# Product-key retrieval in one pass over the table: the marks of the chosen keys, summed as ranks in rows and then turned

## The chip, the cores and the metric

One NeuronCore of a Trainium2 chip runs the whole program. The time is the device time of one execution in microseconds (us); of several executions the median is given. In the profile PE is the matrix engine TensorE (PEld its weight loads), DVE is VectorE, ACT is ScalarE, POOL is GpSimd, SP is SyncE, which here only issues DMAs.

## What is computed

A small network of four layers over 4 sequences of 576 tokens, 64 features each. The change lies in the first layer's feed-forward part, a retrieval with product keys, followed by an attention over what was retrieved:

```python
q = (x @ Wq_pk).reshape(b, n, P, HEADS, DIM_KEY).transpose(2, 0, 1, 3, 4)   # P = 2 sides, 8 heads
sim = jnp.einsum('pbnhd,pkhd->pbnhk', q, pk_keys)                            # 64 keys a side
scores, idx = jax.lax.top_k(sim, PK_TOPK)                                    # 16 a side
index = (idx[0][..., :, None] + 64 * idx[1][..., None, :]).reshape(b, n, HEADS, 256)
score = (scores[0][..., :, None] + scores[1][..., None, :]).reshape(b, n, HEADS, 256)
final_scores, pk_idx = jax.lax.top_k(score, FINAL_TOPK)                      # 16 of the 256 pairs
final_scores = jax.nn.softmax(final_scores, axis=-1)
k = jnp.einsum('bnhk,bnhkd->bnhd', final_scores, keys_table[ind])
v = jnp.einsum('bnhk,bnhkd->bnhd', final_scores, values_table[ind])
```

## The kernel before, in words

The tables are not gathered. `dense_rows_stage` runs over all 64 x 64 pairs of keys of a head as 32 chunks of 128 pairs (`CHUNKS`), with the tokens as columns. The 2304 tokens are 18 tiles of 128, in five groups of 2, 4, 4, 4 and 4 tiles (`GROUP_TILES`); a job is one head of one group, 40 jobs, 1280 chunks. A chunk has 256 columns in group 0 and 512 in the others.

The main loop, per chunk n: `spread_chunk(n)` on TensorE, two bf16 matmuls (L1180, L1181) that spread a token's marks and its logits over the 128 pairs; ScalarE's exponential E (L1289); VectorE's W (L1422), which keeps E where the sum of the two marks is above 16.5; `weigh_chunk(n - 2)` on TensorE, an f32 matmul in two passes (L1191) that adds table rows times W into a PSUM bank. TensorE issues `spread_chunk(n)` only when W(n - 2) is made (`w_made`), and every engine takes its instructions in the order in which they are written. SyncE loads a head's table (2 MB) per job and stacks marks and logits with 32 DMAs per job (`pile`).

The marks say which pairs are chosen. For each token, head and side, a key among the 16 best has a rank; a pair counts when the ranks of its two keys satisfy a limit. VectorE computes them in the generator `choose(t)` for tile t: similarities' maxima, indices and replacements in two rounds (20 steps; L1326, L1331, L1336), the pairs' choice, then for each of 8 heads a comparison that makes a one-hot (key, rank) of both sides (L1376) and a multiplication of the first side (L1380); then the sums and the logits (L1387, L1391, L1393), and, for a group's last tile, the logits less the logarithm of the sums (L1400). `mark(t, h)` on TensorE (L1155) turns and sums: 16 matmuls for each head, one per rank r, with the head's one-hot (128 tokens x 128, every 16th element) as weights and `ranked[:, r, :]`, the identity times 16 - r, as moving operand of 128 columns; they add into a quarter of PSUM bank 6 or 7. ScalarE copies four heads' marks at a time to bf16 (`copy_marks`, L1250). One-hots have two buffers: VectorE starts head h when the marks of head h - 2 are made.

The choice for the next group's tiles runs inside the current group's loop: each tile has a slot of 56 chunks. Within a slot one step of `choose` follows each W from chunk `CHOOSE_AT` = 4 on, the first head's comparison comes at chunk 33 (`ONEHOTS_AT`), head h's at 33 + 2h, TensorE's marks of head h at chunk 36 + 2h (`MARK_AT`), the logarithm at chunk 51 (`LOG_AT`). `project` and `sims` (L1136, L1146) are at chunks 0 and 2; `turn` (L1166) transposes the next job's logits at chunk 4 of each job. So there are 4 slots in group 0's loop, with 256 columns, and 12 in those of groups 1 to 3, with 512. The two tiles of group 0 itself are done ahead of the loop, each with project, similarities, choice and marks one after the other, with nothing beside them.

Of the kernel before, what the change touches and what calls it, by code (L numbers as in the profile page):

```python
# [25 lines left out]
P = 128  # L26
# [974 lines left out]
def dense_rows_stage(nc, core, I, norm, kept):  # L1001
# [7 lines left out]
    with Stage(nc, "pk") as at:  # L1009
# [12 lines left out]
        rest = at.sb("rest", [P, 2 * HEADS, KEYS])  # L1022
        vals = at.sb("vals", [P, 2 * HEADS, TOP])
        ids = at.sb("ids", [P, 2 * HEADS, TOP], U32)
# [11 lines left out]
        onehot = at.sb("onehot", [P, 2, 2, KEYS, TOP], BF16)  # L1036
# [6 lines left out]
        made = at.sb("made", [P, 2, BANK])  # L1043
        (consts, spread_made, xc_made, pk_made, pk_copied, sims_made, sims_copied, shifted, exped, summed, logged,
         onehots, marks_made, marks_copied, split, normal, turned, hi_made, left_made, mid_made, lo_made, x_made, e_made,
         w_made, acc_done, acc_copied, vec) = (at.sem(n) for n in (
            "consts", "spread_made", "xc_made", "pk_made", "pk_copied", "sims_made", "sims_copied", "shifted", "exped",
            "summed", "logged", "onehots_made", "marks_made", "marks_copied", "logits_made", "logits_normal", "logits_turned", "hi_made",
# [26 lines left out]
        with nc.Block() as block:  # L1075
# [53 lines left out]
            def _(pe):  # L1129
# [65 lines left out]
                for t in range(GROUP_TILES[0]):  # L1195
                    project(t)
                    sims(t)
                    for h in range(HEADS):
                        mark(t, h)
                turn(0)  # L1200
                total = len(jobs) * CHUNKS
                for n in range(total):
# [4 lines left out]
                    if t is not None:  # L1207
# [4 lines left out]
                        for h in range(HEADS):  # L1212
                            if i == MARK_AT[h]:
                                mark(t, h)
# [7 lines left out]
            def _(act):  # L1222
# [23 lines left out]
                def copy_marks(t, side):  # L1246
                    g = max(i for i in range(GROUPS_OF) if first_tile[i] <= t)
                    i = t - first_tile[g]
                    act.wait_ge(marks_made, HEADS * t + 4 * side + 4)
                    nc.scalar.activation(marks[:, g % 2, 4 * side:4 * side + 4, i * P:(i + 1) * P],  # L1250
                                         ps[:, 6 + side, :].rearrange("p (h n) -> p h n", n=P), ACT.Copy
                                         ).then_inc(marks_copied, 1)

# [21 lines left out]
                for t in range(GROUP_TILES[0]):  # L1275
# [3 lines left out]
                    copy_marks(t, 0)  # L1279
                    copy_marks(t, 1)  # L1280
# [3 lines left out]
                for n in range(len(jobs) * CHUNKS):  # L1284
# [8 lines left out]
                    if t is not None:  # L1293
# [19 lines left out]
            def _(dve):  # L1313
                steps = Steps(dve, vec)

                def choose(t):
# [7 lines left out]
                    for lo, of in ((0, X), (8, rest)):  # L1324
# [4 lines left out]
                        steps.settle()  # L1329
                        for q in range(2 * HEADS):  # L1330
# [42 lines left out]
                    for h in range(HEADS):  # L1373
                        if HEADS * t + h >= 2:
# [1801 lines left out]
```

## Time and profile before

| what | us |
|---|---|
| median of 3 runs | 4419.82 |
| lowest and highest | 4418.15 and 4446.55 |
| the profiled execution | 4430.5 |
| its span, first to last instruction | 4428.8 |
| PE, DVE, ACT busy in the span | 3578.2, 2649.8, 1444.5 |
| the retrieval's stage in the span (about) | 206 to 2139 |

The rows that follow the change come from that one profiled execution. Times are from the start of its span. A timeline row gives the start, the time that it covers, the engine, the line of the kernel, what is written from what, and how often the same stands in a row; in brackets the idle time ahead of it and what ended it. A matmul's row runs from its start to its modelled end; matmuls overlap, so the time that PE needs for one is read from the distance of starts.

### The profile page before, as it was taken

The page shows a single profiled execution, that of the slowest core. Times are in us where ns is not written, and L with a number is a line of the kernel's source. Part 1 is how long each engine was busy: PE and PEld are TensorE (multiplying, and loading weights), DVE is VectorE, ACT ScalarE, POOL GpSimd, SP SyncE. Part 2 cuts the span into 40 slices and gives each one's busy share as a digit, 9 for nine tenths or more (in the row PEclk, how much of TensorE's full clock was granted, in tenths as well). Part 3 has the DMA queues.
Part 4 walks back from the last instruction along what each step waited for, and adds up shares of the span by engine and source line. Part 5 has one row for each costly group of instructions (what it writes and reads, how often), then busy time and mean ns, then how long its engine had stood idle before and what let it go on. Part 6 is the DMA issues. An engine that isn't in the chain of part 4 may idle for free. (4 is left out here: it accounts for less than half of the span.)

```text
span 4428.8 us, 55552 instructions
## 1 busy us (share of the span) xinstructions
PE 3578.2 (81%) x16818; PEld 2073.3 (47%) x16818; DVE 2649.8 (60%) x7617; ACT 1444.5 (33%) x2746; POOL 351.8 (8%) x354
## 2 busy tenths in 40 slices
PE   5528889999999999999898978866769361899877
PEld 4325554544444454444466645543447241344354
DVE  3368878877887887555334331135455456999812
ACT  2203444444444444444334331013232134100023
POOL 1000000000000000000000001202000000345500
PEclk8569999999999999999879887977779675999968
DMA  0102343444344434444000020000000003100000
GB/s 7 53 10 70 100 99 84 101 89 93 86 100 93 87 82 102 100 111 94 19 20 22 20 85 0 1 4 1 13 19 0 2 0 74 24 0 0 0 7 6
DMA packets 140954, 207.89 MB, mean 47 GB/s; under 512 B 35104, under 2 KB 119657, under 8 KB 135469
## 3 DMA queue, kind: packets, MB, share of 16 engines
q1 hardware_dynamic: 140717, 205.03, 19.4%
q8 instruction: 111, 1.82, 0.2%
q14 instruction: 126, 1.03, 0.1%
HBM read 115.66 MB, written 10.03 MB: 28 GB/s over the span
## 5 line engine op out<-in xcount | busy, mean ns | idle before, releaser
L1191 PE MATMUL psum<-pk_W,pk_kv 128*128 128x512 f32 (+1 forms) x2560 | 1203.9, 552 | 10.0 <-issue 9.8
L1422 DVE SCALAR_TENSOR_TENSOR pk_W<-psum,pk_E 128x512 f32<-128x512 f32 (+1 forms) x1280 | 810.7, 633 | 440.3 <-ACT pk_E L1289 407.3
L1289 ACT ACTIVATE pk_E<-psum 128x512 f32<-128x512 f32 (+1 forms) x1280 | 709.1, 555 | 1004.7 <-PE psum L1181 1002.8
L1191 PEld LDWEIGHTS psum<-pk_W,pk_kv 128*128 128x128 f32 x2560 | 465.4, 191 | 173.7 <-issue 27.0
L1180 PE MATMUL psum<-pk_stack,pk_spread 128*128 128x512 bf16 (+1 forms) x1280 | 462.0, 361 | 90.3 <-DVE pk_W L1422 54.2
L2706 PE MATMUL psum<-tree_w,tree_x 128*128 128x512 bf16 x1728 | 383.4, 380 | 110.9 <-PEq L120 90.5
L1181 PE MATMUL psum<-pk_stack,pk_spread 128*128 128x512 bf16 (+1 forms) x1280 | 459.3, 359 | 0.0
L1180 PEld LDWEIGHTS psum<-pk_stack,pk_spread 128*128 128x128 bf16 x1280 | 125.1, 98 | 445.0 <-DVE pk_W L1422 349.5
L2706 PEld LDWEIGHTS psum<-tree_w,tree_x 128*128 (+1 forms) x1728 | 168.2, 99 | 312.5 <-issue 121.8
L2777 DVE COPY_PREDICATED leaf_acc<-leaf_path,psum 128x512 f32<-128x512 uint32 x468 | 310.2, 728 | 5.3 <-PE psum L2706 2.7
L1181 PEld LDWEIGHTS psum<-pk_stack,pk_spread 128*128 128x128 bf16 x1280 | 125.7, 98 | 241.9 <-issue 232.1
L1155 PEld LDWEIGHTS psum<-pk_ranked,pk_onehot 128*128 128x128 bf16 x2304 | 168.2, 149 | 115.4 <-issue 102.7
L1155 PE MATMUL psum<-pk_ranked,pk_onehot 128*128 128x128 bf16 x2304 | 172.0, 229 | 56.9 <-DVE pk_onehot L1380 56.9
L1125 POOL TENSOR_TENSOR pk_parts<-pk_left,pk_parts 128x512 bf16<-128x512 f32 (+1 forms) x40 | 44.0, 1099 | 1814.9 <-ACT pk_parts L1260 1814.9
L1376 DVE TENSOR_TENSOR pk_onehot<-pk_idf,pk_count 128x2048 bf16<-128x2048 bf16 x144 | 175.4, 1218 | 1.2 <-PE psum L1155 0.6
L295 PE MATMUL psum<-ident,xn 128*64 128x128 f32 x160 | 32.9, 396 | 171.6 <-DVEq L269 157.4
L881 ACT ACTIVATE peer_probs<-peer_probs,peer_stat 128x128 f32<-128x128 f32 (+4 forms) x160 | 96.3, 602 | 219.8 <-DVE peer_stat L916 219.4
L811 PE MATMUL psum<-peer_kv,peer_qT_padded 128*128 128x128 f32 (+4 forms) x320 | 160.4, 594 | 5.9 <-DVE peer_v L986 3.4
L913 DVE CUSTOM_DVE_ANT_0 peer_probs<-psum,peer_mask 128x128 f32<-128x128 f32 (+4 forms) x160 | 85.8, 536 | 113.3 <-PE psum L811 104.2
L1892 PE MATMUL psum<-moe_x,moe_w 128*85 x480 | 112.4, 385 | 43.6 <-PEq L120 42.2
L996 PE MATMUL psum<-peer_v,peer_pT 128*128 128x64 f32 (+2 forms) x960 | 138.5, 287 | 0.0
L2749 POOL TENSOR_TENSOR leaf_acc<-leaf_acc,leaf_of_level 128x512 f32<-128x512 f32 x90 | 90.5, 1039 | 536.6 <-DVE leaf_acc L2777 536.6
(534 smaller groups left out, 4770.2 us busy)
## 6 DMA issues: line engine op xcount, KB each, us to landing
pk_kv<-in_kv SPq DMA_DIRECT2D x40, 2048.0 KB, 8.1
pk_stack<-pk_parts SPq DMA_DIRECT2D x768, 64.0 KB, 2.5
pk_stack<-pk_marks SPq DMA_DIRECT2D x256, 64.0 KB, 2.6
peer_kv<-peer_kept SPq DMA_DIRECT2D x32, 288.0 KB, 2.8
peer_kept<-pk_made SPq DMA_DIRECT2D x32, 256.0 KB, 2.1
tree_weights_x<-in_tree_w SPq DMA_DIRECT2D x32, 256.0 KB, 4.5
pk_stack<-pk_parts SPq DMA_DIRECT2D x192, 32.0 KB, 2.0
dft_cos<-in_cos SPq DMA_DIRECT2D x1, 2596.5 KB
```

The lines of the kernel that those rows point to most:

```text
L811: last = nc.tensor.matmul(ps[0:r, bank, 0:min(w, BANK)], q, self.kT[:, u, 0:min(w, BANK)], start=True, stop=True)
L996: last = nc.tensor.matmul(ps[0:r, 1, c * d:(c + 1) * d], self.pT[0:k, self.pT_at[c] + m * r:self.pT_at[c] + (m + 1) * r], self.v1[0:k, u, ...
L1155: last = nc.tensor.matmul(ps[:, 6 + h // 4, h % 4 * P:(h % 4 + 1) * P], onehot[:, h % 2, :, :, r], ranked[:, r, :], start=(r == 0), stop=( ...
L1180: nc.tensor.matmul(ps[:, n % 2, 0:N], spread[:, 1, c % 2, :], of, start=True, stop=True)
L1181: nc.tensor.matmul(ps[:, 2 + n % 2, 0:N], spread[:, 0, c % 2, :], of, start=True, stop=True).then_inc(x_made, 1)
L1191: nc.tensor.matmul(ps[:, 4, 0:N], kv[:, k % 2, c, :], W[:, n % 3, 0:N], start=(c == 0), stop=(c == CHUNKS - 1)).then_inc(acc_done, 1)
L1289: nc.scalar.activation(E[:, n % 2, 0:width(k)], ps[:, 2 + n % 2, 0:width(k)], ACT.Exp).then_inc(e_made, 1)
L1376: steps.do(nc.vector.tensor_tensor(onehot[:, h % 2, :, :, :], idf[:, :, h, :].unsqueeze(2).to_broadcast([P, 2, KEYS, TOP]), count64[:, :, ...
L1422: nc.vector.scalar_tensor_tensor(W[:, n % 3, 0:width(k)], ps[:, n % 2, 0:width(k)], TOP + 0.5, E[:, n % 2, 0:width(k)], ALU.is_gt, ALU.mul ...
L1892: last = nc.tensor.matmul(ps[0:HALF, 3 * which + u % 3, :], w[:, lo:lo + HALF], x[:, bass.ds(g * BANK, BANK)], start=(k == 0), stop=(k == 2))
L2706: last = nc.tensor.matmul(ps[:, n % BANKS, :], x[:, bass.ds(t * P, P)], w[:, c * BANK:(c + 1) * BANK], start=(k == 0), stop=(k == len(prod ...
L2777: ins = nc.vector.copy_predicated(acc[:, u, level + 1, :, :], over(mask.bitcast(U32), D), bank)
```

## The change

A one-hot is now the moving operand. For each side (half of the heads, `side` 0 or 1) `rank(t, side)` runs 16 matmuls of 512 columns: the weights are `ranked[:, r, :]`, and the moving operand is every 16th element of four heads' one-hots. Their sum is a tile's ranks with the tokens as rows, in bank 6 or 7. ScalarE copies it as bf16 (`copy_ranks`), then `mark(t, side)` transposes the four heads' 128 x 128 blocks, and `copy_marks` copies them as before, from a bf16 PSUM bank. The one-hots have four buffers instead of two, and VectorE waits for the rank step of the half before when it starts a half. The sums and the logits stand between heads 3 and 4 instead of behind head 7. The first rank step stands at chunk 42 of a slot, its transposes at 44; the second at 52 and 54. To make room, `made` and the new `ranks` lie in the memory of `core.xn`, which is free in this stage, `rest` and `ids` in the first two one-hot buffers; before the second tile's and later tiles' indices VectorE waits for the last rank step of the tile before.

```diff
-        onehot = at.sb("onehot", [P, 2, 2, KEYS, TOP], BF16)
+        onehot = at.sb("onehot", [P, 4, 2, KEYS, TOP], BF16)
+        free = core.xn[:, :, :].rearrange("p t d -> p (t d)")
+        made = free[:, 0:2 * BANK].rearrange("p (k n) -> p k n", k=2)
+        ranks = free[:, 2 * BANK:2 * BANK + BANK // 2].bitcast(BF16)
+        rest = onehot[:, 0, :, :, :].rearrange("p s n r -> p (s n r)").bitcast(F32).rearrange("p (q n) -> p q n", n=KEYS)
+        ids = onehot[:, 1, 0, :, :].rearrange("p n r -> p (n r)").bitcast(U32)[:, 0:2 * HEADS * TOP].rearrange("p (q n) -> p q n", n=TOP)
...
-                def mark(t, h):
-                    if h == 0:
+                def rank(t, side):
+                    if side == 0:
                         pe.wait_ge(sims_copied, t + 1)
-                    pe.wait_ge(onehots, HEADS * t + h + 1)
+                    pe.wait_ge(onehots, HEADS * t + 4 * side + 4)
                     for r in range(TOP):
-                        last = nc.tensor.matmul(ps[:, 6 + h // 4, h % 4 * P:(h % 4 + 1) * P], onehot[:, h % 2, :, :, r],
-                                                ranked[:, r, :], start=(r == 0), stop=(r == TOP - 1))
+                        last = nc.tensor.matmul(ps[:, 6 + side, :], ranked[:, r, :],
+                                                onehot[:, :, :, :, r].rearrange("p h s n -> p (h s n)"),
+                                                start=(r == 0), stop=(r == TOP - 1))
+                    last.then_inc(ranks_made, 1)
+
+                def mark(t, side):
+                    pe.wait_ge(ranks_copied, 2 * t + side + 1)
+                    for h in range(4):
+                        last = nc.tensor.transpose(ps[:, 6 + side, :].bitcast(BF16)[:, h * P:(h + 1) * P],
+                                                   ranks[:, h * P:(h + 1) * P], ranked[:, TOP - 1, :])
                     last.then_inc(marks_made, 1)
...
-                        for h in range(HEADS):
-                            if i == MARK_AT[h]:
-                                mark(t, h)
+                        for side in range(2):
+                            if i == RANK_AT[side]:
+                                rank(t, side)
+                            if i == RANK_AT[side] + 2:
+                                mark(t, side)
...
+                def copy_ranks(t, side):
+                    act.wait_ge(ranks_made, 2 * t + side + 1)
+                    if t:
+                        act.wait_ge(marks_made, 2 * t + side - 1)
+                    nc.scalar.activation(ranks[:, :], ps[:, 6 + side, :], ACT.Copy).then_inc(ranks_copied, 1)
...
                     copy_sims(t)
                     exp_top(t)
-                    copy_marks(t, 0)
-                    copy_marks(t, 1)
+                    for side in range(2):
+                        copy_ranks(t, side)
+                        copy_marks(t, side)
...
-                            if i == MARK_AT[4 * side + 3] + 1:
+                            if i == RANK_AT[side] + 1:
+                                copy_ranks(t, side)
+                            if i == RANK_AT[side] + 3:
                                 copy_marks(t, side)
...
+                        if lo == 0 and t:
+                            dve.wait_ge(ranks_made, 2 * t)
                         for q in range(2 * HEADS):
                             steps.add(nc.vector.max_index(ids[:, q, lo:lo + 8], vals[:, q, lo:lo + 8], of[:, q, :]))
...
-                    for h in range(HEADS):
-                        if HEADS * t + h >= 2:
-                            dve.wait_ge(marks_made, HEADS * t + h - 1)
-                        steps.do(nc.vector.tensor_tensor(onehot[:, h % 2, :, :, :],
+                    def mark_head(h):
+                        if h % 4 == 0 and 2 * t + h // 4:
+                            dve.wait_ge(ranks_made, 2 * t + h // 4)
+                        steps.do(nc.vector.tensor_tensor(onehot[:, h % 4, :, :, :],
...
+
+                    for h in range(4):
+                        yield from mark_head(h)
                     dve.wait_ge(exped, t + 1)
...
                     yield
+                    for h in range(4, HEADS):
+                        yield from mark_head(h)
                     if t + 1 in first_tile:
...
-MARK_AT = [ONEHOTS_AT + 2 * h + 3 for h in range(HEADS)]
+RANK_AT = (ONEHOTS_AT + 9, ONEHOTS_AT + 19)
 EXP_AT = ONEHOTS_AT - 1
-LOG_AT = ONEHOTS_AT + 2 * HEADS + 2
+LOG_AT = ONEHOTS_AT + 11
```

## Rows read from the trace of the kernel before

**Rows 1.** The page, busy us of each engine (share of the span) xinstructions
```profile
PE 3578.2 (81%) x16818; PEld 2073.3 (47%) x16818; DVE 2649.8 (60%) x7617; ACT 1444.5 (33%) x2746; POOL 351.8 (8%) x354
```

**Rows 2.** Windows, 512-column loop: us, busy PE, PEld, DVE, ACT, POOL, PEclk, DMA, GB/s
```profile
1500.00:1600.00 100.00, 98.19 (x419) 49.14 (x418) 83.99 (x321) 45.09 (x77) 2.32 (x2) 1.00 0.40 90
```

**Rows 3.** Timeline inside a 512-column slot: start us, us, engine, line, operation, [idle before]
```profile
1640.98 0.38 PE L1180 MATMUL psum<-pk_stack,pk_spread 128*128 128x512 bf16 x1
...
1641.56 1.22 DVE L1376 TENSOR_TENSOR pk_onehot<-pk_idf,pk_count 128x2048 bf16<-128x2048 bf16 x1
...
1642.27 1.17 PE L1155 MATMUL psum<-pk_ranked,pk_onehot 128*128 128x128 bf16 x16
...
1642.81 0.69 DVE L1422 SCALAR_TENSOR_TENSOR pk_W<-psum,pk_E 128x512 f32<-128x512 f32 x1
...
1643.28 0.38 PE L1180 MATMUL psum<-pk_stack,pk_spread 128*128 128x512 bf16 x1
...
1643.42 0.68 DVE L1380 TENSOR_TENSOR pk_onehot<-pk_onehot,pk_depth 128x1024 bf16<-128x1024 bf16 x1
1643.49 0.38 PE L1181 MATMUL psum<-pk_stack,pk_spread 128*128 128x512 bf16 x1
...
1644.54 0.69 DVE L1422 SCALAR_TENSOR_TENSOR pk_W<-psum,pk_E 128x512 f32<-128x512 f32 x1 [0.44 <-ACT pk_E L1289]
1644.57 0.38 PE L1180 MATMUL psum<-pk_stack,pk_spread 128*128 128x512 bf16 x1
```

**Rows 4.** Timeline in the index lookups of the same slot, PE, ScalarE and VectorE
```profile
1605.33 0.60 ACT L1289 ACTIVATE pk_E<-psum 128x512 f32<-128x512 f32 x1 [0.71 <-PE psum L1181]
...
1605.98 0.39 PE L1180 MATMUL psum<-pk_stack,pk_spread 128*128 128x512 bf16 x1
...
1606.62 0.68 DVE L1422 SCALAR_TENSOR_TENSOR pk_W<-psum,pk_E 128x512 f32<-128x512 f32 x1
...
1607.36 0.39 PE L1180 MATMUL psum<-pk_stack,pk_spread 128*128 128x512 bf16 x1
```

**Rows 5.** Timeline inside a 256-column slot of group 0, VectorE and PE
```profile
385.98 1.22 DVE L1376 TENSOR_TENSOR pk_onehot<-pk_idf,pk_count 128x2048 bf16<-128x2048 bf16 x1
...
388.50 1.22 DVE L1376 TENSOR_TENSOR pk_onehot<-pk_idf,pk_count 128x2048 bf16<-128x2048 bf16 x1
...
393.97 0.28 PE L1180 MATMUL psum<-pk_stack,pk_spread 128*128 128x256 bf16 x1
...
394.63 0.27 PE L1180 MATMUL psum<-pk_stack,pk_spread 128*128 128x256 bf16 x1
```

**Rows 6.** Timeline of the first tile, ahead of the main loop
```profile
243.20 3.70 PE L1155 MATMUL psum<-pk_ranked,pk_onehot 128*128 128x128 bf16 x32 [25.39 <-DVE pk_onehot L1380]
...
250.28 0.60 ACT L1250 ACTIVATE pk_marks<-psum 128x512 bf16<-128x512 f32 x1 [10.01 <-PE psum L1155]
...
254.46 1.22 DVE L1376 TENSOR_TENSOR pk_onehot<-pk_idf,pk_count 128x2048 bf16<-128x2048 bf16 x1
...
256.32 0.28 DVE L1387 TENSOR_REDUCE pk_sums<-pk_fvals 128x8 f32<-128x128 f32 x1
...
256.52 0.68 DVE L1391 TENSOR_TENSOR pk_logits<-pk_sim,pk_vals 128x512 f32<-128x512 f32 x1
...
261.49 1.02 ACT L1234 ACTIVATE pk_sim<-psum 128x1024 f32<-128x1024 f32 x1 [2.08 <-PE psum L1146]
```

**Rows 7.** Windows view, 2 us of the first tile, columns as in rows 2
```profile
247.00:249.00 2.00, 1.57 (x16) 1.44 (x16) 1.97 (x4) 0.00 (x0) 0.00 (x0) 0.72 0.00 0
```

**Rows 8.** Source view, loads of the one-hots and of the spread matrix: ns min/median/max
```profile
L1155 PEld LDWEIGHTS psum<-pk_ranked,pk_onehot x2304: 140/148/171, 243.2 to 1748.0; 128*128 128x128 bf16 x192
...
L1180 PEld LDWEIGHTS psum<-pk_stack,pk_spread x1280: 95/98/152, 329.9 to 2134.8; 128*128 128x128 bf16 x183
```

**Rows 9.** Timeline of a later stage, PE, contiguous 128-column bf16 transposes
```profile
3084.94 0.22 PE L2066 MATMUL psum<-rot_soft_ident,rot_attn_q_parts 128*128 128x128 bf16 x1
...
3085.33 0.22 PE L2066 MATMUL psum<-rot_soft_ident,rot_attn_k_parts 128*128 128x128 bf16 x1
```

More of the change, by code:

```diff
@@ L1021, in dense_rows_stage @@
         sim = at.sb("sim", [P, 2, 2 * HEADS, KEYS])
-        rest = at.sb("rest", [P, 2 * HEADS, KEYS])
         vals = at.sb("vals", [P, 2 * HEADS, TOP])
-        ids = at.sb("ids", [P, 2 * HEADS, TOP], U32)
         idf = at.sb("idf", [P, 2, HEADS, TOP], BF16)
@@ L1042, in dense_rows_stage @@
         W = at.sb("W", [P, 3, BANK])
-        made = at.sb("made", [P, 2, BANK])
         (consts, spread_made, xc_made, pk_made, pk_copied, sims_made, sims_copied, shifted, exped, summed, logged,
-         onehots, marks_made, marks_copied, split, normal, turned, hi_made, left_made, mid_made, lo_made, x_made, e_made,
+         onehots, ranks_made, ranks_copied, marks_made, marks_copied, split, normal, turned, hi_made, left_made, mid_made, lo_made, x_made, e_made,
          w_made, acc_done, acc_copied, vec) = (at.sem(n) for n in (
             "consts", "spread_made", "xc_made", "pk_made", "pk_copied", "sims_made", "sims_copied", "shifted", "exped",
-            "summed", "logged", "onehots_made", "marks_made", "marks_copied", "logits_made", "logits_normal", "logits_turned", "hi_made",
+            "summed", "logged", "onehots_made", "ranks_made", "ranks_copied", "marks_made", "marks_copied", "logits_made", "logits_normal", "logits_turned", "hi_made",
             "left_made", "mid_made", "lo_made", "x_made", "e_made", "w_made", "acc_done", "acc_copied", "vector_steps"))
@@ L1211, in _ @@
                             sims(t)
-                        for h in range(HEADS):
-                            if i == MARK_AT[h]:
-                                mark(t, h)
+                        for side in range(2):
+                            if i == RANK_AT[side]:
+                                rank(t, side)
+                            if i == RANK_AT[side] + 2:
+                                mark(t, side)
                     k, c = n // CHUNKS, n % CHUNKS
@@ L1248, in copy_marks @@
                     i = t - first_tile[g]
-                    act.wait_ge(marks_made, HEADS * t + 4 * side + 4)
+                    act.wait_ge(marks_made, 2 * t + side + 1)
                     nc.scalar.activation(marks[:, g % 2, 4 * side:4 * side + 4, i * P:(i + 1) * P],
-                                         ps[:, 6 + side, :].rearrange("p (h n) -> p h n", n=P), ACT.Copy
+                                         ps[:, 6 + side, :].bitcast(BF16)[:, 0:BANK].rearrange("p (h n) -> p h n", n=P), ACT.Copy
                                          ).then_inc(marks_copied, 1)
+                def copy_ranks(t, side):
[3 more added lines that the diff above has]
+                    nc.scalar.activation(ranks[:, :], ps[:, 6 + side, :], ACT.Copy).then_inc(ranks_copied, 1)
                 def split_hi(k):
@@ L1278, in _ @@
                     exp_top(t)
-                    copy_marks(t, 0)
-                    copy_marks(t, 1)
+                    for side in range(2):
+                        copy_ranks(t, side)
+                        copy_marks(t, side)
                 log_sums(0)
@@ L1379, in choose @@
                         yield
-                        nc.vector.tensor_tensor(onehot[:, h % 2, 0, :, :], onehot[:, h % 2, 0, :, :],
+                        nc.vector.tensor_tensor(onehot[:, h % 4, 0, :, :], onehot[:, h % 4, 0, :, :],
                                                 rows_of(depth16[:, h, :], KEYS), ALU.mult).then_inc(onehots, 1)
                         yield
+                    for h in range(4):
+                        yield from mark_head(h)
                     dve.wait_ge(exped, t + 1)
```

1 line of the change is left out of this document (removed).

## The prediction, made before the changed kernel ran

> **What bounds the kernel now.** I read the page's busy times first, then the stretches, then the order of time inside one slot. PE is the busiest engine over the whole program, 81% [rows 1], but that is a mean over many stages. In the retrieval's main loop it is the bound almost alone: 98.19 of 100 us, at the full clock of 2.4 GHz [rows 2]. So in that loop an instruction taken from PE is worth its time, if nothing else comes up behind it.
>
> What stands behind it is seen in the order of time [rows 3]. Two chunks and one head's marks take 3.59 us of PE (1640.98 to 1644.57). A bare chunk takes 1.29 us (1643.28 to 1644.57), so the 16 matmuls of a head's marks take 3.59 - 2 x 1.29 = 1.01 us, 63 ns each. In the same 3.59 us VectorE makes one head's one-hots (1.25 us until the next instruction, then 0.60) and two W's (0.61 each), about 3.1 us, and only then waits 0.44 us. Without the mark between them two chunks are 2.58 us of PE against 3.1 us of VectorE: the marks of before stood exactly where VectorE needed the time. How far VectorE may be late is seen in the index lookups [rows 4]. There it takes 1.37 us a chunk; the W at 1606.62 is 0.69 us behind the end of its E (1605.93), and the spread that waits for it comes 1.38 us after the one before, 0.09 late. So about 0.6 us of lateness is free and the rest is PE's.
>
> In group 0 (256 columns) a chunk without other work is 0.66 us of PE (393.97 to 394.63), but two chunks with a head's one-hots take 2.52 us from one comparison to the next [rows 5], more than 2 x 0.66 + 1.01 = 2.33: VectorE is the bound there and the marks cost nothing.
>
> In the two tiles ahead of the loop everything is one chain. PE starts the marks cold: 32 matmuls in 3.70 us [rows 6], 107 ns each, at half clock, 1.2 GHz; the granted clock of the 2 us from 247 is 0.72 [rows 7], so the full level came at about 248.1, 4.9 us after the start.
>
> **The change part by part.** A tile's 128 matmuls of 128 columns become 32 of 512 columns (16 per rank step, two rank steps) and 8 transposes in bf16; ScalarE copies twice as often. The transposes are of the kind that runs every 56 ns (3084.94 to 3085.33, seven intervals) [rows 9]: 0.25 us a side with its start. ScalarE's extra 2 x 0.6 us [rows 6] lie in chunks where it works 0.6 of 1.29 us, and after the spread that follows the rank step PE has two weighs and a spread to do before it turns, 2.15 us, and ScalarE an exponential and the copy, 0.2 + 0.6 + 0.6 = 1.4: no wait in the loop.
>
> The unknown is the new matmul. A contiguous 512-column one takes 0.21 us of PE (the two spreads of a chunk start at 1643.28 and 1643.49 [rows 3]); that is the low end. But its moving operand is the one-hot at a step of 16 elements, 32 bytes, and no row has such a moving operand. The nearest is the same one-hot as weights [rows 8]: a load takes 148 ns against 98 for contiguous ones, and the pace is 63 ns per 128 columns against 56 [rows 3, 9]. Scaled by columns the pace gives 4 x 63 = 0.25 us, the whole duration of the load 4 x 148 = 0.59 us, the high end; between them lie the two f32 passes of the weigh, half of the chunk's other 0.86 us each, 0.43. I take 0.25, since a pace is what 16 in a row pay: 4.0 us per rank step.
>
> The Trainium skill speaks against the change here: "SBUF — State Buffer" (Door 1) says that reads at full bandwidth need at least two hits in each 16-byte line, so a bf16 step beyond 8 elements pays. The one-hot's slower loads agree in direction; no row shows the rate for a moving operand. It is the second case below.
>
> *Slots of 512 columns* (three groups of four tiles, 12 slots). Off PE: 8 x 1.01 = 8.1 us. Onto PE: 2 x (4.0 + 0.25) = 8.5. And four heads' one-hots now pass with no mark between: VectorE needs 4 x 3.1 = 12.4 us, PE 8 x 1.29 = 10.3; less the free 0.6 that is 1.5 us of PE waiting, twice a slot (the rank step lets VectorE catch up once, after each four), 3.0 us. Net 8.5 + 3.0 - 8.1 = +3.4, times 12 = +41 us.
>
> *Slots of 256 columns* (4). The first rank step starts about 0.9 us after W(40), when head 3 is ready; 4.0 us, then a spread, its semaphore and the E put W(43) 5.7 us after W(40). VectorE has 2.7 us of work for that time (a multiplication at 0.60, two W's at (2.52 - 1.25 - 0.60) / 2 = 0.33, the sums at 0.2, both logits at 0.6), so 3.0 us are new. The second rank step stands in light chunks, where VectorE has about 0.3 us left to do: 4.25 us less that and less the 0.6 that the last mark cost there, +3.4. Together +6.4, times 4 = +26 us.
>
> *The two tiles ahead of the loop.* VectorE reaches head 4 and waits for the first rank step, which can start only after head 3 (before, head 4 asked for head 2's marks); all of the tile's other work on VectorE is queued behind that wait, and the second rank step, the copies and the next tile's similarities wait for it. The step starts cold: 4.9 us at 0.43 us a matmul are 11, the other five at 0.25, 6.0 us in all; the sums and logits brought forward hide 1.4 us of it (0.2 + 0.6 + 0.6, as they are spaced from 256.32 on [rows 6]), 4.8 with the semaphore remain. After head 7 the next tile's similarities (261.49) waited for one mark of 1.2 us; now for a rank step, again cold after the 7.4 us of four heads (4 x 1.86, 254.46 to 256.32), a copy of 0.8 with its release and four slow transposes: 6.0 + 0.8 + 0.5 - 1.2 = +6.1. The second tile pays the same before the logarithm, which ScalarE issues behind its copies. 2 x (4.8 + 6.1) = +22 us.
>
> Other edits: `made`, `ranks`, `rest` and `ids` in borrowed memory change no shape. The wait in front of the second lookup's indices is long met in the loop, and ahead of it covered by the wait for the similarities. With `LOG_AT` earlier, VectorE's wait of about 1 us for the logarithm, once a group, goes; PE did not wait for it, so 0 (at most -4 us).
>
> **Sum.** +41 + 26 + 22 = +89 us. The profiled execution took 4430.5 us, span 4428.8; it would become 4519. The median of the runs is 4419.8, 10.7 lower, so I forecast 4509. With 0.21 us a matmul the three parts are 26 + 21 + 21 = +68 us, 4488.
>
> **The rivals.** About 1%, 44 us, is what a measurement here can tell from no change.
>
> 1. The strided stream runs at half rate, 0.43 us a matmul. For it: the one-hot's loads take half as long again as contiguous ones [rows 8]. Against it: their pace is only an eighth slower. A rank step is 6.9 us: 12 x (2 x 7.15 + 3.0 - 8.1) = 110, the narrow slots 4 x 12.1 = 48, the start 2 x (5.7 + 7.0) = 25. +183, 4603. At 0.59 us, the high end, it would be +279, 4699.
>
> 2. Not slower: VectorE's excess disappears. The place is the eight chunks before each rank step, the price 3.0 us a slot. It needs VectorE to have enough lateness free, 2.1 us instead of 0.6, from where PE's wait is 0, the matmul at 0.21, and the clock up during the first rank steps (3.4 us each). Then 12 x (7.3 - 8.1) = -9, narrow slots 4 x 3 = 12, start 2 x (2.2 + 3.5) = 11: +14, 4434, within 1%. Against it: 0.69 us of lateness already showed [rows 4]. For it: the count of PE's matmul time does go down.
>
> A page's figure would help this rival: the Trainium skill, "TensorE: Matmul & The Clock Gate" (Back-to-back issue gap), gives about 131 ns per sustained 512-column matmul, 2.1 us a rank step, by which rival 2 would come to about 4400. The trace disagrees: contiguous 512-column spreads come 0.21 us apart.
>
> 3. The waits bite in the loop (PE waiting for the copied ranks, VectorE for the rank step at head 4). By the order of issue both are met before they are asked; if the first cost 0.5 us a side, it would be 16 us more on the forecast, 4525, inside its range.
>
> **How the numbers follow.** Forecast with rival 3, 4470 to 4540: 0.50. Half rate or worse: 0.27. Rival 2: 0.15. A gain of over 1% needs -44 us, and the marks are about 8.1 x 12 = 97 us of the bound, so ranks almost free: 0.08. Slower by over 1% takes the first two, less a little: 0.75; within 1% 0.17; faster 0.08. The range holds rival 2's upper part and half rate: 4440 to 4620.
>
> **What would show it.** The new matmuls in the wide slots 0.25 us apart (0.21 or 0.43 decide between the cases). PE waiting for W in the eight chunks before each rank step, with chunks in pairs of 3.1 us; no such wait if rival 2 is right. A VectorE wait for the rank step of about 4 us in each of the first two tiles, and the second tile's similarities about 11 us later than 261.49. A wide slot with its 56 chunks 3.4 us longer than before. The forecast is wrong if wide slots come out shorter, or if PE's wait for W in the loop doesn't grow.

## The result, and the profile after

The changed kernel took 4939.31 us (median of 4 runs, 4937.59 to 4941.75), the one before 4425.59 in runs beside it: a ratio of 1.1161, interval 1.114 to 1.1182. It is some 510 us slower, where +89 was forecast, and it lies far above the range. The profiled execution took 4937.59 us with a span of 4935.7; the mean granted clock fell from 0.881 to 0.840.

The page's busy line, which answers to [rows 1]:

```profile
PE 4034.3 (82%) x15234; PEld 2011.3 (41%) x15234; DVE 2644.3 (54%) x7617; ACT 1463.0 (30%) x2782; POOL 356.8 (7%) x354
```

PE runs 1584 matmuls fewer and is busy 456 us longer. VectorE's and ScalarE's busy times moved by 5.5 and 18.5 us. So the time is in PE's own instructions, and the timeline of PE around a rank step of a wide slot shows in which (start us, us, engine, line, operation, [idle before]); it answers to [rows 3]:

```profile
1717.54 0.39 PE L1190 MATMUL psum<-pk_stack,pk_spread 128*128 128x512 bf16 x1 [0.30 <-DVE pk_W L1451]
1717.77 0.38 PE L1191 MATMUL psum<-pk_stack,pk_spread 128*128 128x512 bf16 x1
1717.98 1.02 PE L1201 MATMUL psum<-pk_W,pk_kv 128*128 128x512 f32 x2
1718.84 14.85 PE L1157 MATMUL psum<-pk_onehot,pk_ranked 128*128 128x512 bf16 x16
1733.51 0.61 PE L1190 MATMUL psum<-pk_stack,pk_spread 128*128 128x512 bf16 x1
...
1736.04 0.63 PE L1190 MATMUL psum<-pk_stack,pk_spread 128*128 128x512 bf16 x1
...
1738.60 0.47 PE L1165 MATMUL psum<-pk_ranked,xn 128*128 128x128 bf16 x4
1738.91 0.38 PE L1190 MATMUL psum<-pk_stack,pk_spread 128*128 128x512 bf16 x1
```

The 16 matmuls with the strided one-hots as moving operand hold PE from 1718.84 to 1733.51: 14.67 us, 0.92 us each. The prediction took 0.25, and its high end was 0.59. The four transposes after them take 0.31 us (0.25 predicted), and the spread at 1717.54 waits for W, as was foreseen.

There is a second thing to see. The chunks at 1733.51 and 1736.04 take 2.53 and 2.56 us, not 1.29. The windows view of the same stretch says why (columns as in rows 2; the seventh number is the granted clock):

```profile
1719.00:1722.00 3.00, 3.00 (x5) 0.35 (x3) 1.67 (x3) 0.00 (x0) 0.00 (x0) 0.95 0.64 100
1722.00:1726.00 4.00, 4.00 (x5) 0.51 (x4) 0.00 (x0) 0.00 (x0) 0.00 (x0) 0.50 0.67 105
1726.00:1730.00 4.00, 4.00 (x6) 0.64 (x5) 0.00 (x0) 0.00 (x0) 0.00 (x0) 0.50 0.26 40
1730.00:1734.00 4.00, 4.00 (x7) 0.59 (x5) 0.00 (x0) 0.00 (x0) 0.00 (x0) 0.50 0.00 0
1734.00:1738.00 4.00, 4.00 (x8) 1.68 (x7) 2.00 (x3) 1.93 (x4) 0.00 (x0) 0.50 0.00 0
1738.00:1742.00 4.00, 3.69 (x14) 1.40 (x13) 1.89 (x4) 3.96 (x6) 0.00 (x0) 0.90 0.00 0
```

PE counts as busy for 4.00 of 4.00 us, and yet the granted clock falls to 0.50, the 1.2 GHz level, during the strided stream, and here it stays there for the two chunks behind it.

In the first tile the chain ahead of the loop shows the same price at both ends of a wait (timeline, several engines):

```profile
251.13 14.85 PE L1157 MATMUL psum<-pk_onehot,pk_ranked 128*128 128x512 bf16 x16 [30.97 <-DVE pk_onehot L1404]
266.02 1.23 DVE L1400 TENSOR_TENSOR pk_onehot<-pk_idf,pk_count 128x2048 bf16<-128x2048 bf16 x1 [13.63 <-PE psum L1157]
...
273.62 14.85 PE L1157 MATMUL psum<-pk_onehot,pk_ranked 128*128 128x512 bf16 x16 [6.33 <-DVE pk_onehot L1404]
```

VectorE waits there for 13.63 us; some 4.8 were predicted.

**The ledger.** ScalarE copies each tile's similarities once, 18 times in all; the distance from one copy to the next is the length of a slot, and it sorts the whole difference by place. Means, in us, from ScalarE's timeline:

| distance between copies | before | after | difference |
|---|---|---|---|
| tile 0 to 1 and tile 1 to 2, ahead of the loop | 43.6, 76.4 | 76.1, 105.8 | 32.5 + 29.4 = 62 |
| narrow slot (256 columns), three alike | 63.1 | 93.8 | 4 slots: 121 |
| wide slot (512 columns), nine alike | 87.1 | 114.8 | 27.7, times 12 = 332 |

The sum is 515 us. The last copy of the retrieval's accumulator stands at 2138.4 before and 2655.3 after, 517 later; what follows it takes 2290.4 before and 2280.4 after, to the end of each span.

### The profile page after: what moved, and what is told of

The parts are those of the page before. It is cut to its first block and busy times, and to the rows that moved or that the text cites. A ratio compares the mean times of both kernels' runs of the same rounds, so it can differ in the third digit from the quotient of the medians.

```text
span 4935.7 us, 52471 instructions
## 1 busy us (share of the span) xinstructions
PE 4034.3 (82%) x15234; PEld 2011.3 (41%) x15234; DVE 2644.3 (54%) x7617; ACT 1463.0 (30%) x2782; POOL 356.8 (7%) x354
## 5 line engine op out<-in xcount | busy, mean ns | idle before, releaser
L1201 PE MATMUL psum<-pk_W,pk_kv 128*128 128x512 f32 (+1 forms) x2560 | 1240.1, 567 | 7.9 <-issue 7.8
L1157 PE MATMUL psum<-pk_onehot,pk_ranked 128*128 128x512 bf16 x576 | 534.5, 1096 | 74.5 <-DVE pk_onehot L1404 74.5
L1190 PE MATMUL psum<-pk_stack,pk_spread 128*128 128x512 bf16 (+1 forms) x1280 | 475.6, 372 | 123.9 <-DVE pk_W L1451 86.8
L1201 PEld LDWEIGHTS psum<-pk_W,pk_kv 128*128 128x128 f32 x2560 | 481.5, 197 | 180.8 <-issue 34.9
L1191 PE MATMUL psum<-pk_stack,pk_spread 128*128 128x512 bf16 (+1 forms) x1280 | 472.4, 369 | 0.0
L1157 PEld LDWEIGHTS psum<-pk_onehot,pk_ranked 128*128 128x128 bf16 x576 | 69.2, 121 | 491.7 <-issue 477.8
L1400 DVE TENSOR_TENSOR pk_onehot<-pk_idf,pk_count 128x2048 bf16<-128x2048 bf16 x144 | 175.4, 1218 | 27.9 <-PE psum L1157 27.3
L1921 PE MATMUL psum<-moe_x,moe_w 128*85 x480 | 113.7, 388 | 43.6 <-PEq L120 42.2
L996 PEld LDWEIGHTS psum<-peer_v,peer_pT 128*128 128x128 f32 (+2 forms) x960 | 122.4, 200 | 20.0 <-issue 14.6
```

Of the source, the lines that this page charges most:

```text
L996: last = nc.tensor.matmul(ps[0:r, 1, c * d:(c + 1) * d], self.pT[0:k, self.pT_at[c] + m * r:self.pT_at[c] + (m + 1) * r], self.v1[0:k, u, ...
L1157: last = nc.tensor.matmul(ps[:, 6 + side, :], ranked[:, r, :], onehot[:, :, :, :, r].rearrange("p h s n -> p (h s n)"), start=(r == 0), st ...
L1190: nc.tensor.matmul(ps[:, n % 2, 0:N], spread[:, 1, c % 2, :], of, start=True, stop=True)
L1191: nc.tensor.matmul(ps[:, 2 + n % 2, 0:N], spread[:, 0, c % 2, :], of, start=True, stop=True).then_inc(x_made, 1)
L1201: nc.tensor.matmul(ps[:, 4, 0:N], kv[:, k % 2, c, :], W[:, n % 3, 0:N], start=(c == 0), stop=(c == CHUNKS - 1)).then_inc(acc_done, 1)
L1400: steps.do(nc.vector.tensor_tensor(onehot[:, h % 4, :, :, :], idf[:, :, h, :].unsqueeze(2).to_broadcast([P, 2, KEYS, TOP]), count64[:, :, ...
```

## The experiments

All changes are against the changed kernel unless it is said otherwise. For comparison by place, the same slot lengths for every kernel, in us, from its profiled execution. The three medians of the kernel before belong to the changed kernel, to the contiguous, ladder and grouped versions, and to the last four:

| kernel | tiles 0, 1 | narrow | wide | median | ratio to before |
|---|---|---|---|---|---|
| before | 43.6, 76.4 | 63.1 | 87.1 | 4425.59, 4431.3 and 4427.16 | |
| after | 76.1, 105.8 | 93.8 | 114.8 | 4939.31 | 1.1161 (1.114 to 1.1182) |
| contiguous rank steps | 54.1, 86.8 | 68.9 | 89.0 | 4483.46 | 1.0114 (1.0091 to 1.0136) |
| a ladder of steps | 64.4, 94.6 | 80.4 | 100.7 | 4689.42 (one run) | |
| old marks, grouped | 53.3, 86.9 | 69.9 | 89.8 | 4497.65 | 1.0153 (1.0127 to 1.0179) |
| rank steps at step 2 | 56.7, 87.4 | 70.1 | 90.3 | 4508.98 (three of four) | 1.0191 (1.016 to 1.0221) |
| step 2, per two heads | 47.2, 77.4 | 65.4 | 87.3 | 4435.87 | 1.0023 (1.0006 to 1.004) |
| the same, wide slots only | 43.7, 76.4 | 63.8 | 87.3 | 4428.85 | 1.001 (0.9995 to 1.0025) |
| old marks at step 2 | 43.7, 76.6 | 63.8 | 86.3 | 4420.59 | 0.9992 (0.9979 to 1.0004) |

### The rank steps with a contiguous moving operand

This leaves the change whole (its grouping, waits, copies and transposes) and takes only the stride away. Each matmul reads 512 neighbouring elements of the one-hots, which are not the marks of one rank.

```diff
-    onehot[:, :, :, :, r].rearrange("p h s n -> p (h s n)"),
+    onehot[:, :, :, :, :].rearrange("p h s n r -> p (h s n r)")[:, r * BANK:(r + 1) * BANK],
```

> The changed kernel with one difference: each of the 16 rank matmuls of 512 columns streams 512 elements that lie side by side in the one-hot buffers, instead of every 16th one. The counts, shapes, waits and order are those of the changed kernel; the marks no longer hold the ranks, so the choice of pairs is another. Theory A (the step of 32 bytes in the moving operand is what costs 0.92 us a matmul): the matmuls start 0.21 us apart at the full clock, a rank step is 3.4 us instead of 14.7, the two slow chunks behind it and the half clock during it go, a 512-column slot takes about 89 us (before 87.2, after 115.5), and the kernel takes 4485 to 4500, still 60 to 80 us above the kernel before. Rival B (the form itself costs: new weights for every 512 columns, adding into one bank, or VectorE and the DMAs working on the same memory beside it): they stay 0.9 us apart and the kernel near 4935. Rival C (A is right and grouping four heads costs nothing): near 4420.

It took 4483.46 us, beside 4431.3 for the kernel before in the same comparison. PE's timeline around a rank step, and two windows over it and over the chunks behind:

```profile
1524.02 3.62 PE L1157 MATMUL psum<-pk_onehot,pk_ranked 128*128 128x512 bf16 x16
1527.47 0.38 PE L1190 MATMUL psum<-pk_stack,pk_spread 128*128 128x512 bf16 x1
```

```profile
1524.00:1527.40 3.40, 3.40 (x17) 1.55 (x16) 2.09 (x5) 0.00 (x0) 0.00 (x0) 1.00 0.63 95
1527.40:1530.00 2.60, 2.60 (x10) 1.15 (x8) 1.27 (x2) 1.68 (x3) 0.00 (x0) 1.00 0.63 102
```

The step takes 3.45 us, 0.216 a matmul, the clock stays at 1.00, and 456 of the 514 us are gone. So the stride is the cause of both, the long matmuls and the lost clock. (The marks are other ones here; the version with a step of 2 below makes the right ones and keeps the clock as well.) The rest, +52 us, is what the change costs with a free stride, and it splits as the prediction had it: 21 us in the first two tiles (21 predicted with 0.21 us a matmul), 21 in the narrow slots (21), and 1.9 a wide slot, 23 in twelve (26). The narrow slots lose it as was foreseen, by VectorE standing idle until the first W behind each rank step (timeline of one of them):

```profile
472.25 0.42 DVE L1451 SCALAR_TENSOR_TENSOR pk_W<-psum,pk_E 128x256 f32<-128x256 f32 x1 [2.37 <-ACT pk_E L1309]
...
487.19 0.42 DVE L1451 SCALAR_TENSOR_TENSOR pk_W<-psum,pk_E 128x256 f32<-128x256 f32 x1 [3.68 <-PE psum L1201]
```

Together that is 65 us of slots; the first copy of similarities came 2 us earlier, and the stages behind the retrieval took 2281.8 us in this execution, 9 less than before. Those stages took 2279 to 2301 us in the profiles of this study, and no version changes their code, so 9 us there is most likely scatter.

### A ladder of steps

Here the 16 matmuls of a rank step read the same data with 16 different patterns: steps of 1, 1, 2, 2, 4, 4, 8, 8, 16 and 16 elements, then twice two neighbours out of every 16, twice four out of every 32, then steps of 12 and 6. What comes out has no meaning as marks.

```diff
+    flat = onehot[:, :, :, :, :].rearrange("p h s n r -> p (h s n r)")
+    step = (1, 1, 2, 2, 4, 4, 8, 8, 16, 16, 0, 0, 0, 0, 12, 6)[r]
+    if step:
+        of, to = flat[:, 0:step * BANK:step], ps[:, 6 + side, :]
...
```

> The changed kernel with the 16 matmuls of each rank step reading the one-hot buffers at different steps, two in a row of each: step 1, 2, 4, 8, 16 elements of 2 bytes; then two that read 2 neighbours every 16 elements, two that read 4 neighbours every 32, and one each at step 12 and 6. The marks are no longer ranks. The distance of starts of each gives its price. Theory A1 (a line of 16 bytes read once costs the same however much of it is used, and at least two hits in a line hide it): steps 1, 2 and 4 at 0.21 us, 8 perhaps between, 16 and 12 at 0.92, two neighbours per line about 0.46 or less. A2 (price grows with the bytes passed over): 0.06 us per element of step, so 0.21, 0.21, 0.23, 0.46, 0.92. A3 (only neighbours are fast, any step above 1 pays the full price): all but step 1 at 0.92. The kernel as a whole lies between 4500 and 4750 by A1 or A2 and near 4900 by A3.

One execution: 4689.42 us. The matmuls of one rank step one by one, from PE's timeline in short windows; the distance of two starts is what a matmul takes of PE:

```profile
1015.87 0.38 PE L1167 MATMUL psum<-pk_onehot,pk_ranked 128*128 128x512 bf16 x1
...
1016.75 0.61 PE L1167 MATMUL psum<-pk_onehot,pk_ranked 128*128 128x512 bf16 x1
1017.18 0.63 PE L1167 MATMUL psum<-pk_onehot,pk_ranked 128*128 128x512 bf16 x1
1017.64 1.08 PE L1167 MATMUL psum<-pk_onehot,pk_ranked 128*128 128x512 bf16 x1
1018.54 1.08 PE L1167 MATMUL psum<-pk_onehot,pk_ranked 128*128 128x512 bf16 x1
1019.44 1.10 PE L1167 MATMUL psum<-pk_onehot,pk_ranked 128*128 128x512 bf16 x1
1020.36 1.10 PE L1167 MATMUL psum<-pk_onehot,pk_ranked 128*128 128x512 bf16 x1
1021.27 0.64 PE L1167 MATMUL psum<-pk_onehot,pk_ranked 128*128 128x512 bf16 x1
1021.74 0.64 PE L1167 MATMUL psum<-pk_onehot,pk_ranked 128*128 128x512 bf16 x1
...
1022.51 0.63 PE L1167 MATMUL psum<-pk_onehot,pk_ranked 128*128 128x512 bf16 x1
1022.94 1.08 PE L1167 MATMUL psum<-pk_onehot,pk_ranked 128*128 128x512 bf16 x1
1023.84 0.86 PE L1167 MATMUL psum<-pk_onehot,pk_ranked 128*128 128x512 bf16 x1
1024.52 0.40 PE L1184 MATMUL psum<-ident,pk_logits 128*128 128x128 f32 x1
```

The first four (steps 1 and 2) take 0.88 us together, 0.22 each. Step 4 takes 0.43 and 0.46, step 8 takes 0.90 twice, step 16 0.92 and 0.91, two neighbours out of 16 take 0.47, step 12 0.90, step 6 0.68. What these have in common is the number of 16-byte lines that a partition's 512 elements touch: 256 lines at step 4 and with two neighbours out of 16, 384 at step 6, 512 at steps 8, 12 and 16. All come to 1.7 to 1.8 ns a line. A longer line would make step 8 cheaper than step 16, and a shorter one would make step 4 as dear as step 8; neither is so. Step 2 touches 128 lines, which at that price is 0.23 us, just above the matmul's own 0.22: over the 32 rank steps of the loop the medians are 0.227 us at step 2 and 0.216 at step 1. So theory A1 holds but for its two hits; A2 (0.46 at step 8) and A3 (0.92 from step 2 on) fall.

The windows view parts the stride from the clock:

```profile
1015.80:1019.40 3.60, 3.60 (x9) 0.83 (x8) 0.69 (x1) 0.01 (x1) 0.00 (x0) 1.00 0.90 382
1019.40:1021.20 1.80, 1.80 (x3) 0.23 (x2) 0.00 (x0) 0.00 (x0) 0.00 (x0) 1.00 0.02 9
1021.20:1022.90 1.70, 1.70 (x5) 0.50 (x4) 0.00 (x0) 0.00 (x0) 0.00 (x0) 0.84 0.00 0
1022.90:1024.50 1.60, 1.60 (x3) 0.35 (x2) 0.00 (x0) 0.00 (x0) 0.00 (x0) 0.50 0.00 0
```

A step of 16 at clock 1.00 (0.92 us) costs what step 12 costs at 0.50 (0.90 us) and what step 16 cost in the changed kernel, where the matmuls at 1.00 and those at 0.50 both start 0.918 us apart (medians over the loop). Four neighbours out of every 32, by contrast, which touch 128 lines, took 0.43 us at 0.50 (1022.51 to 1022.94), the half-clock price of 512 columns (4 x 107 ns by [rows 6]). The price of a line does not hang on the clock, so the low clock is not why the strided stream is slow; and since the contiguous rank steps kept 1.00, it is the strided stream that the clock falls in. The windows also rule out the transfers: with a DMA share of 0.90 the contiguous and half-price steps ran at their own pace, and step 16 took 0.92 us with 0.02.

The expectation was wrong in part: step 4 was thought free. The Trainium skill, "SBUF — State Buffer" (Door 1), says that two hits in each 16-byte line are enough and that a bf16 step of 8 elements is free. Its unit, the 16-byte line, is what the measured steps follow; its threshold isn't. Step 4 has two hits a line and took twice the contiguous time; step 8 has one hit and took four times. Step 2, with four hits, took 5% over the contiguous time; three were not tried.

### The old marks, four heads at a time

The opposite cut: the changed kernel with the marks of the kernel before. One-hots are weights again, 128 marks a tile, but they wait for four heads and are issued together at the places of the rank steps. There are no copied ranks and no transposes; the four buffers, the borrowed memory and the sums and logits between heads 3 and 4 stay as in the changed kernel.

```diff
-    last = nc.tensor.matmul(ps[:, 6 + side, :], ranked[:, r, :],
-                            onehot[:, :, :, :, r].rearrange("p h s n -> p (h s n)"),
-                            start=(r == 0), stop=(r == TOP - 1))
+    for h in range(4):
+        for r in range(TOP):
+            last = nc.tensor.matmul(ps[:, 6 + side, h * P:(h + 1) * P], onehot[:, h, :, :, r],
+                                    ranked[:, r, :], start=(r == 0), stop=(r == TOP - 1))
...
```

> The changed kernel's order, four one-hot buffers, places in the slot and waits, but with the marks made as before: for each of four heads 16 matmuls of 128 columns with the one-hot as weights, 64 in one go at chunk 42 and 64 at chunk 52, no rank copies and no transposes. TensorE's work is that of the kernel before. Theory A: grouping alone costs, since VectorE needs 3.1 us for two chunks with a head's one-hots and TensorE now only 2.6: 3.0 us a slot of 512 columns (36 in all), 4 to 6 us a slot of 256 columns (25 in all), and 9 to 10 us in each of the two first tiles, where head 4 waits for four heads' marks: +80 us, near 4500, and a 512-column slot of 90 us. Rival (VectorE has enough lateness free): only the two first tiles cost, 4435 to 4445, and a slot of 87 us.

4497.65 us, 1.0153. The groups view, the spreads that open a chunk, in the kernel before, in the contiguous version and in this one (busy us, mean ns | idle before, what ended it):

```profile
L1180 PE MATMUL psum<-pk_stack,pk_spread 128*128 128x512 bf16 (+1 forms) x1280 | 462.0, 361 | 90.3 <-DVE pk_W L1422 54.2
L1190 PE MATMUL psum<-pk_stack,pk_spread 128*128 128x512 bf16 (+1 forms) x1280 | 462.8, 362 | 128.7 <-DVE pk_W L1451 91.4
L1183 PE MATMUL psum<-pk_stack,pk_spread 128*128 128x512 bf16 (+1 forms) x1280 | 463.0, 362 | 132.0 <-DVE pk_W L1432 95.2 <-DMA pk_stack<-pk_marks 33.3
```

PE waits 95.2 us for W, where the kernel before waited 54.2 in the same group. With TensorE's instructions those of the kernel before, the new order costs what the contiguous version costs or a little more, and in the same places: +10 in each of the first two tiles, +6.8 a narrow slot, +2.7 a wide one. That it is the grouping and not the four buffers or the borrowed memory is shown by the last experiment, which keeps both and loses nothing. The new place of the sums and logits has no run of its own.

### Rank steps with a layout that they can read

The one-hots' layout is turned to (pair of ranks, head, side, key, rank in pair), so that a rank's elements lie at a step of 2. VectorE makes a head's one-hots in two comparisons of half the size (683 ns each, 1217 before for the whole).

```diff
-onehot = at.sb("onehot", [P, 4, 2, KEYS, TOP], BF16)
+onehot = at.sb("onehot", [P, TOP // 2, 4, 2, KEYS, 2], BF16)
...
-    onehot[:, :, :, :, r].rearrange("p h s n -> p (h s n)"),
+    onehot[:, r // 2, :, :, :, r % 2].rearrange("p h s n -> p (h s n)"),
```

> The changed kernel with the one-hots laid out as (pair of ranks, head, side, key, rank within the pair), so that the rank matmul reads 512 elements at a step of 2 (4 bytes) and everything else stays: same sums, same order, same waits. VectorE's comparison of a head is two instructions of 1024 elements, whose innermost run is 2 elements. Theory A (only the 16-byte lines that the moving operand touches cost, and step 2 touches 128 of them, which the stream hides): matmuls 0.21 to 0.22 us apart, rank steps 3.5 us, the kernel within 10 us of e1_contiguous (4483), if VectorE keeps its pace. If VectorE loses its double pace on runs of 2, its comparison takes 2.1 us instead of 1.2 and the kernel goes to 4560 to 4600. Rival (the matmul's form costs): near 4930.

The matmuls run nearly as the contiguous ones, 387 ns each (379 there) and 0.227 us from start to start (0.216 there), and with the right ranks the clock stays up in the loop too:

```profile
1500.00:1600.00 100.00, 95.20 (x317) 41.54 (x316) 84.04 (x338) 43.92 (x77) 2.63 (x2) 1.00 0.40 89
```

Three of its four executions took 4502.65 to 4517.56 us, median 4508.98, some 25 above the contiguous version, where at most 10 were expected. (The fourth took 15351.91 us; it is left out here, nothing on record explains it, and the median of all four is 4513.27.) Where the 25 went is in the groups of this kernel: PE waits for W 107.5 us instead of 91.4, the wide slot is 1.3 longer and the narrow one 1.2. Two things can make that up. The split comparison gives VectorE 0.15 us more a head (2 x 683 - 1217 ns), 1.2 a slot, in slots where it is already late by the grouping; and the 32 matmuls of a slot at 0.227 instead of 0.216 us are 0.35. The slots come to some 24 us more in all. How the two share it is not shown.

### Rank steps of two heads

With the same layout, four rank steps a tile, each after two heads and with 256 columns, so that VectorE is let catch up twice as often. The sums and the logits are behind head 7 again.

```diff
-RANK_AT = (ONEHOTS_AT + 9, ONEHOTS_AT + 19)
+RANK_AT = [ONEHOTS_AT + 4 * p + 5 for p in range(4)]
...
-    pe.wait_ge(onehots, HEADS * t + 4 * side + 4)
+    pe.wait_ge(onehots, HEADS * t + 2 * p + 2)
```

> The layout of f1_step2, with a rank step per two heads (16 matmuls of 256 columns, four steps a tile, at chunks 38, 42, 46 and 50), so that the four buffers work as two pairs and VectorE does the next two heads while TensorE sums two; sums and logits behind head 7 again, the logarithm at chunk 51. Theory A (VectorE's excess over TensorE between the rank steps is what remains of the loss): per four chunks TensorE has 5.2 + 1.7 us and VectorE 6.2, so a 512-column slot falls to 86.5 us (before 87.2, e1 89.2); the 256-column slots cost 0 to 1 us over before and the first two tiles 2 to 5 us each. Together within 10 us of the kernel before. Rival (the excess is elsewhere, grouping has no part): the slot stays near 89 and the kernel near 4480.

4435.87 us, 1.0023. Its groups view:

```profile
L1205 PE MATMUL psum<-pk_stack,pk_spread 128*128 128x512 bf16 (+1 forms) x1280 | 462.3, 361 | 100.9 <-DVE pk_W L1488 65.9 <-DMA pk_stack<-pk_marks 33.6
...
L1172 PE MATMUL psum<-pk_onehot,pk_ranked 128*128 128x256 bf16 x1152 | 145.4, 278 | 60.6 <-DVE pk_onehot L1442 60.6
```

The wait for W falls from 107.5 to 65.9 us and with it the wide slot from 90.3 to 87.3: the smaller groups take the waits away again. (The sums and logits moved in the same run; but in the contiguous version the long chunks, 1.76 us every second one as in the timeline further below, stand where one-hots are made.) But a slot of 87.3 is 0.8 above the 86.5 that was expected, and no shorter than before. Sixteen matmuls of 256 columns span 1.98 us in PE's timeline, so with 0.27 for the last they start (1.98 - 0.27) / 15 = 0.114 us apart: 57 ns per 128 columns, where the old marks paid 63. That and the transposes leave little to win: 64 x 0.114 + 2 x 0.25 = 7.8 us a tile against 8.1.

The same with the first six tiles left at marks per head, so that only wide slots have rank steps (against the version above):

```diff
-PAIRS_FROM = 0
+PAIRS_FROM = 6
```

> f2_pairs for the 12 tiles whose slots have 512 columns; for the first six tiles, where TensorE is not the bound, marks per head as in the kernel before (one-hot as weights, now at a step of 2), no rank copies there. By theory A the wide slots are 86.5 us as in f2 and the rest costs what it did before: 4405 to 4420 us beside about 4428 for before. Rival: no gain over before beyond 0.1%.

4428.85 us, 1.001 (0.9995 to 1.0025): no gain, where 4405 to 4420 us were expected. The first two tiles are as before again (43.7 and 76.4), the wide slots stay at 87.3. The expected gain would have had to come from wide slots shorter than before, and there were none.

### Only the layout

Marks per head as before in all tiles, one-hots as weights, but read at a step of 2 and held in four buffers, with the borrowed memory (against the version above).

```diff
-PAIRS_FROM = 6
+PAIRS_FROM = 18
```

> The kernel before's marks per head and order for all tiles; what differs is the layout of the one-hots (step 2 instead of 16 within the weights), four buffers instead of two, and the borrowed memory. Theory A says that lines also set the pace of the weight loads: 63 ns per matmul fall to the 56 ns of contiguous ones, a head's marks from 1.01 to 0.90 us, a 512-column slot by 0.8 to 0.9 us, the kernel by 8 to 12 us, about as much as f3. Rival (the 63 ns are something else, such as f32 PSUM adding): no change, 4425 to 4435. VectorE's split comparison may take 0.05 us more a head, hidden in the wide slots.

The source view of the line with the marks:

```profile
L1163 PEld LDWEIGHTS psum<-pk_ranked,pk_onehot x2304: 96/98/152, 241.1 to 1739.2; 128*128 128x128 bf16 x192
L1163 PE MATMUL psum<-pk_ranked,pk_onehot x2304: 216/219/314, 241.1 to 1739.2; 128*128 128x128 bf16 x192
```

The loads fall from 148 ns [rows 8] to 98, those of contiguous weights, and the wide slot falls by 0.8 us, as expected. The total is 4420.59 us against 4427.16, a ratio of 0.9992 (0.9979 to 1.0004), where 8 to 12 us less were expected. The narrow slots give 0.7 us each back, most likely since VectorE is the bound there and its comparison now comes in two parts. It is the lowest median of the study and is not told apart from the kernel before; no version here beats the kernel before.

## Why the prediction was wrong

The direction was right and the size was not. Step by step:

- *The price of the strided matmul failed.* "The nearest is the same one-hot as weights" was the step. From it came 0.25 us by pace and 0.59 by duration; the runs show 0.92. The weights' rows could not bound it: in the trace of before a load of 128 columns at a step of 16 went by at 63 ns, beside other work, while the same pattern as moving operand costs 0.92 us per 512 columns, 230 ns per 128. As a high end 4 x 148 ns looked safe, and it had no claim to be: the row of one operand bounds the other from neither side. The low end, 0.21 us, was right: 0.216 with a contiguous operand.
- The rule of the Trainium skill, "SBUF — State Buffer" (Door 1), had been weighed in the prediction as what spoke against the change, and its case was priced at half rate, 0.43 us. The measured 0.92 is beyond that, since a step of 16 elements puts every element on a line of its own; the ladder shows half rate where two elements share one.
- *The clock was missed.* No step or rival had PE's clock fall in the loop. It falls to 0.50 during each rank step of the loop and is back 2 to 5 us behind its end. In the mean of the 24 rank steps in wide slots, the two chunks behind one take 2.50 and 2.14 us, where the contiguous version has 1.29 and 1.57 (the second holds the transposes): 1.8 us a step, 3.6 a wide slot. The stream itself pays nothing for the low clock, as the ladder shows. Per wide slot, 2 x (14.8 + 0.2) for the rank steps and transposes, + 3.6 for the clock, - 8.1 for the marks make 25.5 of the 27.7 measured, which leaves 2.2 for the waits.
- *The grouping was right, its price a little high.* Chunks in pairs of 3.1 us before a rank step were predicted. ScalarE's timeline of the changed kernel:

```profile
1712.07 0.60 ACT L1309 ACTIVATE pk_E<-psum 128x512 f32<-128x512 f32 x1 [1.17 <-PE psum L1191]
1713.36 0.60 ACT L1309 ACTIVATE pk_E<-psum 128x512 f32<-128x512 f32 x1 [0.69 <-PE psum L1191]
1715.12 0.60 ACT L1309 ACTIVATE pk_E<-psum 128x512 f32<-128x512 f32 x1 [1.17 <-PE psum L1191]
1716.41 0.60 ACT L1309 ACTIVATE pk_E<-psum 128x512 f32<-128x512 f32 x1 [0.69 <-PE psum L1191]
```

  They come 1.29 and 1.76 us apart in turn, 3.05 a pair. Both halves of the cut agree: with a contiguous operand +1.9 us a wide slot (2.2 by the prediction's sum at 0.21), and with no rank steps at all +2.7. The waits alone, predicted at 3.0 a slot, are 2.2 in the changed kernel (above) and 2.6 in the contiguous version, where the rank steps and transposes take 7.4 and the marks took 8.1.
- *The narrow slots and the first two tiles* were right in their mechanism and sized right at 0.21 us: 21 and 21 us measured with the contiguous operand, with VectorE's waits of 2.37 and 3.68 us behind the rank steps of a narrow slot and of 8.1 us in the first two tiles together (4.8 each predicted). With the real one VectorE's wait in the first tile is 13.63 us instead of 4.8, and the whole price of the step falls through, 30 us a narrow slot, since a rank step there has little beside it.
- *Rival 1*, half rate, was the right mechanism at half its size. *Rival 2* fell: in the contiguous version, with the stride free and the clock at 1.00, the wait for W was 91.4 us against 54.2 and the time 1.0114. *Rival 3*, waits in the loop for the copied ranks, did not show. Of the transposes' wait for the copied ranks the groups have 2.8 us in the whole kernel, and of VectorE's wait for a rank step 27.3, 2 x 13.6, both in the first two tiles:

```profile
L1165 PE MATMUL psum<-pk_ranked,xn 128*128 128x128 bf16 x144 | 16.6, 247 | 2.8 <-ACT xn L1271 2.8
L1400 DVE TENSOR_TENSOR pk_onehot<-pk_idf,pk_count 128x2048 bf16<-128x2048 bf16 x144 | 175.4, 1218 | 27.9 <-PE psum L1157 27.3
```

With 0.92 us in the prediction's own sum the three parts are 12 x (2 x (14.7 + 0.25) + 3.0 - 8.1) = 298, 4 x (6.4 + 2 x 10.7) = 111, and 2 x (4.8 + 6.1) + 4 x (14.7 - 6.0) = 57: +466 us. The clock behind the rank steps, 3.6 us a wide slot or 43, brings it to 509, of 515 measured in the slots.

## What to carry to other kernels

An operand's role on PE is part of its price: the layout that cost 63 ns per 128 columns as weights cost 230 as the moving operand, so before two operands change places, count how many 16-byte lines the new moving operand touches in a partition (about 1.8 ns each here, in bf16). Where no row shows an operation in its role, a row of another role is not a bound, and the range has to say so. And work taken off PE in small pieces between chunks may have been what gave VectorE its time: gathered into pieces of four heads it cost 1 to 2% here with contiguous operands, with the old marks and at a step of 2 alike; in pieces of two heads it cost 0.2%.

## What was not expected of the hardware

- A strided moving operand costs by 16-byte lines, 0.90 to 0.92 us for 512 lines, 0.68 for 384 and 0.43 to 0.47 for 256. The price of 512 lines was the same at clock 1.00 and at 0.50. A step of 2 bf16 elements costs 0.227 us, neighbours 0.216.
- The granted clock can fall to 0.50 while PE counts as busy without a gap (4.00 of 4.00 us from 1722), and the instructions behind pay for it: up to 2.53 us a chunk instead of 1.29.
- As weights the same stride is far cheaper: 148 ns a load at a step of 16, 98 at a step of 2, and 0.8 us of 87.1 in a wide slot for 128 such loads.
- Contiguous 512-column bf16 matmuls in a row come 0.216 us apart, 16 of them here as well as 57 in a later stage of the kernel before, (12.47 - 0.38) / 56:

```profile
3791.28 12.47 PE L2706 MATMUL psum<-tree_w,tree_x 128*128 128x512 bf16 x57
```
